# Layer 0 of a two-layer conditioned attention kernel, its per-step order rearranged: both outputs one step later, a transpose between the query projections, probabilities ahead of the values

## The reference, cut to what matters

```
xn = layer_norm(x, norm_w, norm_b)
q, k, v = xn @ q_w + q_b, xn @ k_w + k_b, (xn @ v_w + v_b) * mask
att = softmax(q k^T + mask_bias)          # per head, 128 x 128
y = att v
h = layer_norm(y, w2, b2) * (1 + scale) + shift   # scale, shift from the condition
x = x + silu(h) @ out_w + out_b
```

## Time and profile before

| | before |
|---|---|
| median of 3 runs | 1081.39 us (1081.2 to 1085.8) |
| the profiled execution's own time | 1081.82 us |
| span of that execution in the trace | 1080.0 us |
| mean granted TensorE clock | 0.998 |
| PE busy | 1042.5 us (97%), 8632 matmuls |
| PE weight loads | 905.0 us (84%) |
| DVE, ACT, POOL busy | 762.5, 614.2, 423.6 us (71%, 57%, 39%) |

### The profile page before, as it was taken

One profiled execution on the slowest core, in us unless ns is written; L12 is line 12 of the kernel. 1 busy time (PEld: TensorE's weight loads), 2 busy tenths in 40 slices (PEclk: granted clock), 3 DMA queues, 4 the chain that ended last, 5 costly groups with the idle time before them and its releaser, 6 DMA issues. The chain is left out here.

```text
span 1080.0 us, 25940 instructions
## 1 busy us (share of the span) xinstructions
PE 1042.5 (97%) x8632; PEld 905.0 (84%) x8632; DVE 762.5 (71%) x1354; ACT 614.2 (57%) x2024; POOL 423.6 (39%) x746
## 2 busy tenths in 40 slices
PE   5999999999999999999998899999999999999996
PEld 4878888988888888888887788888888888888885
DVE  4656666676667766676569787877777777777775
ACT  4366668766687667766596653444444444444343
POOL 1232443433433434334433444443444344444423
PEclk9999999999999999999999999999999999999999
DMA  9824110111012110211112212222111111112111
GB/s 294 243 86 143 43 54 32 63 51 53 32 54 63 41 61 24 63 63 43 36 53 93 95 45 65 64 65 63 63 51 49 54 55 53 56 60 63 44 39 40
DMA packets 47937, 73.21 MB, mean 68 GB/s; under 512 B 10352, under 2 KB 16624, under 8 KB 47888
## 3 DMA queue, kind: packets, MB, share of 16 engines
q1 hardware_dynamic: 47888, 72.59, 21.2%
HBM read 55.76 MB, written 16.81 MB: 67 GB/s over the span
## 5 line engine op out<-in xcount | busy, mean ns | idle before, releaser
L468 POOL TENSOR_SCALAR stat<-stat 128x1 f32<-128x1 f32 x128 | 35.3, 276 | 492.8 <-DVE stat L921 452.7
L1338 PE MATMUL bank<-xt_hi,w_hi 128*128 128x256 f32 x768 | 223.3, 291 | 3.0 <-DVE xt_lo L930 3.0
L1339 PE MATMUL bank<-xt_lo,w_hi 128*128 128x256 f32 x768 | 218.5, 284 | 0.0
L1340 PE MATMUL bank<-xt_hi,w_lo 128*128 128x256 f32 x768 | 218.3, 284 | 0.0
L633 ACT ACTIVATE prob<-prob,neg_max 128x128 f32<-128x128 f32 x512 | 198.5, 395 | 7.0 <-DVE neg_max L944 6.9
L1338 PE MATMUL bank<-w_hi,xt_hi 128*128 128x512 f32 x384 | 157.0, 409 | 0.9 <-DVE w_lo L872 0.9
L1338 PEld LDWEIGHTS bank<-xt_hi,w_hi 128*128 128x128 f32 x768 | 148.4, 193 | 10.5 <-DVE w_lo L872 4.7
L1340 PE MATMUL bank<-w_hi,xt_lo 128*128 128x512 f32 x384 | 150.5, 392 | 0.0
L1339 PE MATMUL bank<-w_lo,xt_hi 128*128 128x512 f32 x384 | 149.8, 390 | 0.0
L1339 PEld LDWEIGHTS bank<-xt_lo,w_hi 128*128 128x128 f32 x768 | 148.5, 193 | 1.1
L1340 PEld LDWEIGHTS bank<-xt_hi,w_lo 128*128 128x128 f32 x768 | 148.4, 193 | 0.0
(11 more groups left out here) (124 smaller groups left out, 2189.7 us busy)
## 6 DMA issues: line engine op xcount, KB each, us to landing
x_in<-in_x_dram SPq DMA_DIRECT2D x32, 256.0 KB, 2.8
x_res<-in_x_dram SPq DMA_DIRECT2D x32, 256.0 KB, 3.0
between_layers<-x_res SPq DMA_DIRECT2D x32, 256.0 KB, 2.0
x_in<-between_layers SPq DMA_DIRECT2D x32, 256.0 KB, 3.0
x_res<-between_layers SPq DMA_DIRECT2D x30, 256.0 KB, 2.6
out_dram<-x_res SPq DMA_DIRECT2D x30, 256.0 KB, 2.0
room<-in_L_cond_W_emb_dram SPq DMA_DIRECT2D x8, 512.0 KB, 7.5
prob<-in_L_cond_emb_w_dram SPq DMA_DIRECT2D x4, 512.0 KB, 7.3
```

The source lines that it names most:

```text
L468: pool.tensor_scalar(v[:, 8:9], v[:, 7:8], EPS, None, ALU.add).then_inc(s[a_in].sem, 1)
L1338: pe.matmul(o, a_hi, b_hi, start=start, stop=False)
L1339: pe.matmul(o, a_hi, b_lo, start=False, stop=False)
L1340: return pe.matmul(o, a_lo, b_hi, start=False, stop=stop)
```

## The change

It is a change of order alone: the arithmetic and the number of instructions stay. On TensorE, `turn_yn` of the second sequence moves from the end of a step to the next one, between the two halves of the query projection; `output` of the first sequence moves from the end of its step to the next step's place between `scores(k, 1)` and `turn_probs(k, 0, (2, 3))`, and `output` of the second from there to the place after `y_rows(k, 0)`; `turn_probs(k, 1, (2, 3))` goes ahead of `values(f, 0)`, and `weigh(k, 1)` ahead of `turn_yn(k, 0)`. The lists of the other engines follow. On ScalarE, `tanh` of the late sequence stands behind `exps(k, 0, (0,))` and ahead of `exps(k, 0, (1,))`, and its `s_high` behind `exps(k, 0, (3,))`. On GpSimd, its `add_shift` opens the step. On SyncE the stores and the reloads of the residual rows are put off to match, and step 16 takes over one transpose and one output more. In step 0, `film(1, 6)` goes from the end of the step to the place after `weigh(k, 1)`. Banks are dealt anew for `H` and `O`.

```
-        FIRST = dict(..., H=(6, 7), O=(5, 6))
+        FIRST = dict(..., H=(6, 5), O=(6, 7))
...
 (ScalarE, step0)
+                exps(k, 0, (0,))
                 if late:
                     tanh(late + (-1), 1)
-                exps(k, 0, (0,))
-                if late:
-                    s_high(late + (-1), 1)
                 exps(k, 0, (1,))
...
                 exps(k, 0, (3,))
+                if late:
+                    s_high(late + (-1), 1)
                 q_out(f, slot, 1)
...
                 y_t_out(k, 1)
+                xt_high(n, 1 - slot, 0)
+                xt_high(n, 1 - slot, 1)
                 tanh(k, 0)
-                xt_high(n, 1 - slot, 0)
-                xt_high(n, 1 - slot, 1)
                 s_high(k, 0)
...
 (VectorE, step0, the new list; step 0 and G - 3, G - 2 extras left out)
+                softmax(k, 0, (0, 1))
+                film_scale(late + (-1), 1)
+                softmax(k, 0, (2, 3))
+                silu(late + (-1), 1)
+                stats1(n, 0)
+                softmax(k, 1, (0,))
+                s_low_part(late + (-1), 1)
+                softmax(k, 1, (1, 2))
+                output(FIRST, late + (-1), 0)
+                softmax(k, 1, (3,))
                 stats1(n, 1)
                 sums_inverse(k, 0)
                 y_norm(0, k, 1 - slot, 0)
+                output(FIRST, late + (-1), 1)
                 sums_inverse(k, 1)
                 v_add(0, FIRST, f, slot, 0)
                 film_scale(k, 0)
+                xt_low(n, 1 - slot, 0)
+                xt_low(n, 1 - slot, 1)
+                y_norm(0, k, 1 - slot, 1)
                 silu(k, 0)
-                y_norm(0, k, 1 - slot, 1)
                 s_low_part(k, 0)
-                xt_low(n, 1 - slot, 0)
-                xt_low(n, 1 - slot, 1)
                 v_add(0, FIRST, f, slot, 1)
-                output(FIRST, k, 0)
...
 (TensorE, step0)
                 scores(k, 1 - slot, 0)
                 queries0(f, slot, 0)
+                if late:
+                    turn_yn(0, late + (-1), 1)
                 queries0(f, slot, 1)
                 turn_probs(k, 0, (0, 1))
                 scores(k, 1 - slot, 1)
                 if late:
-                    output(0, FIRST, late + (-1), 1)
+                    output(0, FIRST, late + (-1), 0)
                 turn_probs(k, 0, (2, 3))
                 keys(0, f, slot, 0)
                 weigh(k, 1 - slot, 0)
                 turn_probs(k, 1, (0, 1))
                 y_rows(k, 0)
+                if late:
+                    output(0, FIRST, late + (-1), 1)
                 keys(0, f, slot, 1)
+                turn_probs(k, 1, (2, 3))
                 values(0, FIRST, f, slot, 0)
-                turn_probs(k, 1, (2, 3))
+                weigh(k, 1 - slot, 1)
                 turn_yn(0, k, 0)
-                weigh(k, 1 - slot, 1)
                 turn(n, 0)
                 turn(n, 1)
                 y_rows(k, 1)
                 values(0, FIRST, f, slot, 1)
-                output(0, FIRST, k, 0)
-                turn_yn(0, k, 1)
...
 (GpSimd, step0)
+                if late:
+                    add_shift(late + (-1), 1)
                 norm1(n, 0)
+                norm1(n, 1)
                 residual(0, k, 0)
-                norm1(n, 1)
                 norm2(k, 0)
-                residual(0, k, 1)
                 v_mask(f, slot, 0)
                 add_shift(k, 0)
                 norm2(k, 1)
+                residual(0, k, 1)
                 v_mask(f, slot, 1)
-                add_shift(k, 1)
```

More of the change, by code:

```diff
@@ L1095, in step0 @@
             def step0(i, n, f, k, late, slot):
+                softmax(k, 0, (0, 1))
                 if late:
                     film_scale(late + (-1), 1)
+                if i == 0:
+                    film(0, 5)
+                softmax(k, 0, (2, 3))
+                if late:
+                    silu(late + (-1), 1)
+                stats1(n, 0)
+                softmax(k, 1, (0,))
+                if late:
+                    s_low_part(late + (-1), 1)
+                softmax(k, 1, (1, 2))
+                if late:
+                    output(FIRST, late + (-1), 0)
+                if i == 0:
+                    embed_sum(1, 0, 6)
                 if i == G - 3:
                     spread_norm_b(1)
[L1100 to L1114, removed]
                 softmax(k, 1, (3,))
@@ L1155, in step_mixed @@
                 stats1(n, 0)
-                softmax(k, 1, (0, 1, 2))
-                output(FIRST, late + (-1), 1)
+                softmax(k, 1, (0,))
+                s_low_part(late + (-1), 1)
+                softmax(k, 1, (1, 2))
+                output(FIRST, late + (-1), 0)
                 softmax(k, 1, (3,))
@@ L1537, in step0 @@
                     bias_sum(1, WK, 6, True)
-                turn_probs(k, 1, (2, 3))
+                weigh(k, 1 - slot, 1)
+                if i == 0:
+                    film(1, 6)
                 turn_yn(0, k, 0)
-                weigh(k, 1 - slot, 1)
                 if i == G - 2:
```

88 lines of the change are left out of this document (37 added, 51 removed).

## The result

The changed kernel takes 1100.59 us (median of 4 runs, 1099.38 to 1101.79), against 1082.18 us for the kernel before in its runs; the ratio is 1.0161, with a 95% interval from 1.0143 to 1.018. It is slower, as forecast, by 1.6%. The median is 0.6 us from the 1100.0 forecast; the forecast was made against the profiled execution, and that took 1101.79 us, 1.8 from it. The sum behind the figure hit less well than the figure: two of its terms were off by 6 and 8 us in opposite directions, and the trace tells both.

The account below looks back on a forecast made before the run. TensorE was taken as the bound, with some 0.86 us of wait a step. Each step was to change by 2.3 + 0.1 - 0.86 = +1.54 us, fourteen by +21.6; 1081.82 + 21.6 - 3.4 = 1100.0 us, range 1084 to 1108.

Parts of the forecast that it names:

- What the change removes: In each loop step, the waits of weigh(k, 1) (0.61 us) and output(k, 0) (0.25) go: -0.86 us a step.
- The wait that it adds: In each loop step, TensorE waits at turn_probs(k, 0, (1,)) and has lost 2.3 us by weigh(k, 0), bounds 1.75 and 2.65.
- the links: From turn_yn through film_scale, add_shift, tanh and exponentials to turn_probs: 5.06 us, against 3.80 us of other work on TensorE.
- the term of 9.99 us for ScalarE's stretch: From the start of exps(k, 0, (1,)) to the last copy for weigh(k, 0), ScalarE works 9.99 us without a gap.
- The ends of layer 0: Step 0, the wait behind step 14 and step_mixed: together -3.4 us, bounds -4.5 and 0.
- the 1.6 us of step 0: In step 0, the 1.6 us for which the scores of step 1 wait behind film(1, 6) are won.
- the 0.9 us for split weights: Behind step 14, the wait of 0.9 us for the split weights goes, since output(late, 1) now lies ahead of it.
- as no worse: step_mixed already has the new wait in the kernel before, 1.45 us at the same transposes, and was taken as no worse.
- Faster: the cover holds: Rival: in each step the whole chain fits under TensorE's 3.80 us of work; 14 us won, 1068 us; chance 0.07.
- ACT catches up: Rival: part of ScalarE's 9.99 us is hidden waiting, so only 1.26 us a step stay; +3.6, 1085 us; chance 0.08.
- The late DVE feeds on itself: Rival: full bounds of a step, and step_mixed waits longer for VectorE's key sums ahead of weigh; +28, 1110 us; chance 0.12.
- The clock falls: Rival: stops bring 1.2 GHz for one half of the queries in each step; 41 us on top, 1141 us; chance 0.02.

Follow-up runs that it names:

- The first experiment's kernel: The changed kernel with the late tanh on ScalarE moved behind exps(k, 0, (1,)), in step0 and step_mixed: 1078.85 us, ratio 0.9953 to the kernel before.
- the kernel with the wait of 3.88 us: The changed kernel with the late turn_yn on TensorE moved behind both halves of the query projection, in step0 alone: 1160.84 us, ratio 1.0724 to the kernel before.

## Why the prediction was right, and where it was not

**What the change removes** was right in place and size. The first experiment's kernel keeps every part of the change but the place of the `tanh`: its step is 34.03 us, of which 0.31 is idle at `weigh`; 33.7 us are left, as 34.43 - 0.86 + 0.1 = 33.67 had it. That includes the +0.1 for the switches, which had no row and which no run shows by itself.

**The wait that it adds** was right in mechanism and somewhat too large. The chain from `turn_yn` to `turn_probs` took 5.31 us (199.35 - 194.04), where the links summed to 5.06 plus 0.4 for VectorE. Link by link in the step after: to `film_scale` 230.69 - 229.54 = 1.15 (forecast 0.73 + 0.4, and indeed VectorE came to it straight from the second maxima); to `add_shift` 0.94 (0.89); to `tanh` 1.09 (1.22); to the exponentials 0.53 (0.53). By `weigh` TensorE is at 207.96 - 194.04 = 13.92 us, where 12.14 + 2.3 = 14.44 was taken and 13.89 was the lower bound. The step that failed is the term of 9.99 us for ScalarE's stretch: it was read as work without a gap, since no bracket stood in it. After, the stretch from 233.25 to 242.80 + 0.60 is 10.15 us with `s_high` (0.53) in it, so 9.6 without. Nearly all of the missing 0.4 us lies at two copies: in the kernel before, `prob_turned` starts 0.88 and 0.89 us behind the `q_out` ahead of it (233.08 to 233.96, 238.01 to 238.90), after, 0.71 and 0.72 (234.79 to 235.50, 240.06 to 240.78). Those were waits of ScalarE for `turn_probs`, too short to be shown as idle time; now the transposes are done when ScalarE comes to them. The 0.15 for the signal from the copies to `weigh` had no row; after, the last copy ends at 243.40 and `weigh` starts at 243.54, 0.14 later. So +1.12 us a step instead of +1.54: 14 x 1.12 = 15.7 us, where the sum had 21.6.

**The ends of layer 0** were wrong in sign: -3.4 forecast, about +4 found. Taking the start of step 1's scores and of `step_mixed`'s scores as marks: step 0 ends 87.16 - 83.61 = 3.55 us earlier, but 3.35 of that is one output (2.82) and one `turn_yn` (0.53) that were only moved on, so it wins 0.2 instead of 2.5. Three things go against it: 0.71 us of wait at the new place of `turn_probs`, the wait for `film_ab` of 0.90, which did not go but moved to `turn_yn`, and the lower clock, which lay behind the mark before (0.50 from 87.9 to 91.3) and lies ahead of it now (77.2 to 80.6).

Steps 1 to 14 take 503.85 us instead of 486.93 (587.46 - 83.61, and 574.09 - 87.16 in the trace before): 16.9 more, 1.2 beyond the regular steps. In this, step 1 is better by 1.8 without that lower clock, and step 14 is worse by 2.3 (39.85 us against 36.43, with 1.12 of that in every step), about the wait at `step_mixed`'s scores. From there to the end it is 1100.0 - 587.46 = 512.54 instead of 505.91 us, 6.6 more. Of that, 46.20 - 41.77 = 4.4 lie ahead of the first turned keys of step 16, with one moved `turn_yn` (0.53) in them. The moved output costs next to nothing: it falls into step 16, where the kernel before had waits (0.81, 0.55 and 0.75 us in its timeline), and that step is only 0.3 longer. The last 32.03 - 30.08 = 1.9 are the tail, whose lists did not change, at a clock of 0.89 in place of 1.00; the two kernels with fewer or earlier low parts have 30.1 there.

So the steps of the prediction that failed are these: the 1.6 us of step 0, of which 0.9 moved to `turn_yn` instead of going; the 0.9 us for split weights, which in the kernel before lies at 606.85, at the query weights of `step_mixed`, and after is still there, 1.05 us at 625.77; and `step_mixed` "as no worse". For the last, it was asked what the moved output would cover in its new place and not what it had covered in its old one, the end of step 14, where VectorE is late. Step 14 and `step_mixed` lose 2.3 + 4.4 - 0.5 = 6.2 us by the marks. Of these, 46.20 - 45.06 = 1.1 go with the `tanh` (first experiment), and 4.1 come back when six low parts are left out and the clock stays up. How much of the 4.1 the moved output had covered before stays open: the kernel before was not run without these low parts, and from the early split the changed order gains only 0.6 us more than it. Nor are the low parts all: a wait of 1.3 us at the scores is left in both edits, and it ends on `bias_wide`, which the changed list of VectorE also puts behind the two `xt_low` and `y_norm`. That rival was not tried.

**The rivals.** "Faster: the cover holds" is what the steps became as soon as the `tanh` no longer stood between the exponentials, though with 1078.85 in place of 1068 by the sum, since the ends don't win there either. "ACT catches up" was half true (the 0.4 us above). "The late DVE feeds on itself" did not happen: VectorE's lateness is the 0.4 us of the links and no more. "The clock falls" I gave 2 in 100, for every step; it did not fall in the steps, but it did at the start of `step_mixed`, within the second of two waits of 2.14 and 2.45 us, and in the steps of the kernel with the wait of 3.88 us. One row with a wait of 1.45 us said nothing of longer ones, and the trace before has a row on the other side: at the wait of 1.6 us ahead of step 1 the clock falls to 0.50.

**The total.** 21.6 - 3.4 = +18.2 was forecast and +20.0 found in the profiled span, as 15.7 from the steps and 4.3 from the ends. That the figure was met this closely is luck: two errors offset each other. The direction and the mechanism were right by themselves.

## What to carry to other kernels

Where an in-order engine works for two chains, a call of the late chain goes behind all the calls of the urgent chain that are ready before it: one instruction that waits 1.6 us between two groups of exponentials cost 1.5 us in each of fourteen steps, and with the call one place further on that cost was gone. When work is moved, price what it will cover in its new place and also what it covered in the old one, on every engine that had its slack there. A part of a rearrangement may be a loss by itself (here +2.8%) and pay only with the others, so a part's gain read from one wait holds only if nothing else in the step gets nearer to its producer.

## What the runs showed of the hardware

How long TensorE visibly stood still does not by itself tell whether the granted clock fell. It stayed at 1.00 in steps with a stop of 1.40 us in each 35.55, and in `step_mixed` before with stops of 1.45 and 1.84 us. It fell to 0.50 within a stop of 3.88 us, within the second of two stops of 2.14 and 2.45 us, right behind one stop of 2.13 us in the first experiment's kernel (565.4 to 572.3), behind a stop of 1.6 us in the kernel before (87.9 to 91.3), within one of 0.90 us in step 0 after (77.2 to 80.6), and, in the kernel with the key weights split early, behind stops of only 0.94 and 0.88 us. What tells these apart these runs leave open. And a stretch of ScalarE without a bracket in the timeline held about 0.4 us of waiting.
